# First attention of a decoder layer: each step's values product in two halves of 256 queries, one half and one unit of maxima behind each pair of scores

## The reference, cut to what is touched

```python
attn = jnp.einsum('bhqd,bhkd->bhqk', q, k) * SCALE
diff = pos[None, :] - pos[:, None]
diff = jnp.where(diff > 0, 0.0, diff)
attn = attn + diff[None, :, :] * slopes[:, None, None] * MAX_BIAS
w = jax.nn.softmax(attn, axis=-1)
out = jnp.einsum('bhqk,bhkd->bhqd', w, v)
```

## Time and profile before

| | us |
|---|---|
| median of 3 runs | 1965.26 (1962.78 to 1966.6) |
| the profiled execution | 1962.87 |
| its span, first to last instruction | 1961.1 |
| of it the 16 groups of the first attention | some 766 (160 to 926) |

### The profile page before, as it was taken

One profiled execution on the slowest core, in us unless ns is written; L12 is line 12 of the kernel. 1 busy time (PEld: TensorE's weight loads), 2 busy tenths in 40 slices (PEclk: granted clock), 3 DMA queues, 4 the chain that ended last, 5 costly groups with the idle time before them and its releaser, 6 DMA issues. The chain is left out here.

```text
span 1961.1 us, 37426 instructions
## 1 busy us (share of the span) xinstructions
PE 1681.3 (86%) x15124; PEld 1148.3 (59%) x15124; DVE 1374.4 (70%) x2318; ACT 994.8 (51%) x1602; POOL 475.1 (24%) x312
## 2 busy tenths in 40 slices
PE   8758999999999999997584898875993999999970
PEld 7734444444444444442573776764772888999970
DVE  7687888888888888880675878762332777777736
ACT  5325777777777777776252545452442433333310
POOL 6440000000000000000432633320453344444430
PEclk9957999999999999999797999987996999999995
DMA  7877444444444444400654112103212343333225
GB/s 248 222 198 183 65 65 65 68 65 65 65 65 65 65 65 64 65 9 10 209 197 137 65 55 75 54 11 135 77 52 81 96 91 92 89 90 90 36 31 173
DMA packets 128567, 178.93 MB, mean 91 GB/s; under 512 B 30144, under 2 KB 95056, under 8 KB 127380
## 3 DMA queue, kind: packets, MB, share of 16 engines
q1 hardware_dynamic: 114964, 154.57, 34.4%
q0 software_dynamic: 13440, 22.07, 5.4%
HBM read 110.49 MB, written 69.47 MB: 92 GB/s over the span
## 5 line engine op out<-in xcount | busy, mean ns | idle before, releaser
L638 DVE TENSOR_REDUCE att_row_max<-att_ring 128x2 f32<-128x1024 f32 x512 | 602.2, 1220 | 108.9 <-PE att_ring L704 57.1
L622 ACT ACTIVATE att_w_exp<-att_s_ps 128x512 f32<-128x512 f32 x1024 | 548.2, 596 | 232.3 <-PE att_s_ps L747 157.3
L774 PE MATMUL att_a_ps<-att_w_exp,att_v_group 128*32 128x512 f32 x2048 | 273.6, 606 | 0.2 <-ACT att_w_exp L622 0.2
L733 PE MATMUL att_s_ps<-att_q_stack,att_k_stack 62*128 62x512 f32 x640 | 182.0, 481 | 0.0
L560 POOL COPY att_eyes<-keep_slope_eye 128x384 bf16<-128x384 bf16 x16 | 8.1, 510 | 641.9 <-PE att_s_ps L747 632.6
L733 PEld LDWEIGHTS att_s_ps<-att_q_stack,att_k_stack 62*128 62x128 f32 x640 | 84.4, 184 | 124.0 <-ACT att_w_exp L622 113.0
L2050 POOL DMA_INDIRECT x_scr<-ex_y,ex_home x64 | 105.1, 1642 | 181.2 <-DVE ex_y L2139 166.6
L2094 ACT ACTIVATE ex_hid<-ex_h_ps,ex_b 128x512 f32<-128x512 f32 x128 | 87.3, 686 | 115.5 <-DVE ex_h_lo L2149 61.9
L704 PE MATMUL att_ring<-att_k_stack,att_q_stack 60*128 60x512 f32 x640 | 131.5, 451 | 6.2 <-DVE att_att L665 3.2
L747 PE MATMUL att_s_ps<-att_eyes,keep_past_bf 64*128 64x64 bf16 x3840 | 133.8, 193 | 0.0
L2149 DVE TENSOR_TENSOR ex_h_lo<-ex_hid,ex_h_hi 128x512 fp32r<-128x512 f32 x128 | 130.5, 1019 | 4.4
(11 more groups left out here) (270 smaller groups left out, 3810.2 us busy)
## 6 DMA issues: line engine op xcount, KB each, us to landing
first_w_raw<-ew SPq DMA_DIRECT2D x16, 1024.0 KB, 7.5
att_k_stack<-qk_scr SPq DMA_DIRECT2D x120, 128.0 KB
keep_k_stack<-qk_scr SPq DMA_DIRECT2D x72, 128.0 KB
rows_scr<-att_zeros POOLq DMA_DIRECT2D x8, 1040.0 KB, 22.9
ex_rows<-rows_scr SPq DMA_DIRECT2D x16, 520.0 KB, 4.8
cr_q<-q_scr SPq DMA_DIRECT2D x16, 512.0 KB, 5.3
att_q_stack<-qk_scr SPq DMA_DIRECT2D x60, 128.0 KB
qk_scr<-qkv_t_hi SPq DMA_DIRECT2D x7, 1024.0 KB, 4.3
```

The source lines that it names most:

```text
L622: nc.scalar.activation(w_exp[(STEPS * g.n + st) % SETS][h][:, :], s_ps[v % BANKS][:, :], ACT.Exp).then_inc(exp_done, 1)
L638: nc.vector.tensor_reduce(out, ring[place.slot][:, :, :], AX.X, ALU.max).then_inc(ring_free, 1)
L733: ins = nc.tensor.matmul(s_ps[v % BANKS][:, :], ks[g.buf][rows, c, j, kt * P:(kt + 1) * P], qs[g.buf][rows, j, c * CH:(c + 1) * CH], start ...
L774: ins = nc.tensor.matmul(a_ps[32 * h:32 * h + 32, :], vg[g.buf][:, kt, h * VW:h * VW + 32], w_exp[(STEPS * g.n + st) % SETS][h][:, :], sta ...
```

## The change

`values` gets a parameter `part`. For `kt == 0` part 0 does the whole block as before (512 columns) and part 1 does nothing; for the other seven key tiles of a chunk each part multiplies 256 of the 512 query columns, and the step is counted on `pv_done` by the last one. `old_values` chooses the group as before. In the step, part 0 follows the first pair of scores (with the transpositions behind it), then comes the first unit of maxima, then the second pair of scores, part 1, and the second unit. ScalarE's accumulator copies in steps 1 and 9 move from behind head 1's exponential to behind head 2's, because the last values now end later. Nothing else differs; the ring's order is the same.

```diff
-                        if st == 1 and h == 1 and has_last:
+                        if st == 1 and h == 2 and has_last:
                             copy_acc(g.plus(-1), 1)
-                        if st == 9 and h == 1:
+                        if st == 9 and h == 2:
                             copy_acc(g, 0)
...
-            def values(g, st):
+            def values(g, st, part):
                 c, kt = divmod(st, KT)
-                pe.wait_ge(exp_done, TILES * g.n + 4 * st + 4 + BANKS)
-                if st == 0:
-                    pe.wait_ge(v_ready, g.n + 1)
-                if kt == 0:
-
-                    pe.wait_ge(acc_done, 2 * g.n + c + 1)
+                if part == 0:
+                    pe.wait_ge(exp_done, TILES * g.n + 4 * st + 4 + BANKS)
+                    if st == 0:
+                        pe.wait_ge(v_ready, g.n + 1)
+                    if kt == 0:
+                        pe.wait_ge(acc_done, 2 * g.n + c + 1)
+                elif kt == 0:
+                    return
+                cols = slice(0, CH) if kt == 0 else slice(part * CH // 2, (part + 1) * CH // 2)
                 for h in range(HG):
-                    ins = nc.tensor.matmul(a_ps[32 * h:32 * h + 32, :], vg[g.buf][:, kt, h * VW:h * VW + 32],
-                                           w_exp[(STEPS * g.n + st) % SETS][h][:, :], start=(kt == 0), stop=(kt == KT - 1))
-                ins.then_inc(pv_done, 1)
+                    ins = nc.tensor.matmul(a_ps[32 * h:32 * h + 32, cols], vg[g.buf][:, kt, h * VW:h * VW + 32],
+                                           w_exp[(STEPS * g.n + st) % SETS][h][:, cols], start=(kt == 0), stop=(kt == KT - 1 and part == 1))
+                if kt == 0 or part == 1:
+                    ins.then_inc(pv_done, 1)
+
+            def old_values(g, st, has_last, part):
+                if st > 1:
+                    values(g, st - 2, part)
+                elif has_last:
+                    values(g.plus(-1), STEPS + st - 2, part)
...
                     score_pair(g, st, 0)
-                    if st > 1:
-                        values(g, st - 2)
-                    elif has_last:
-                        values(g.plus(-1), STEPS + st - 2)
+                    old_values(g, st, has_last, 0)
...
+                    if with_max:
+                        max_pair(n, 2 * st, PLACES[g.n, "max", 2 * st])
                     score_pair(g, st, 2)
+                    old_values(g, st, has_last, 1)
                     if with_max:
-                        for i in range(2):
-                            max_pair(n, 2 * st + i, PLACES[g.n, "max", 2 * st + i])
+                        max_pair(n, 2 * st + 1, PLACES[g.n, "max", 2 * st + 1])
...
             for st in (STEPS - 2, STEPS - 1):
-                values(last, st)
+                for part in range(2):
+                    values(last, st, part)
```

## The result

| | before | after |
|---|---|---|
| median, us | 1964.41 (4 runs, 1962.78 to 1966.6) | 1980.76 (4 runs, 1976.27 to 1982.43) |
| profiled execution, us | 1962.87 | 1982.43 |
| its span, us | 1961.1 | 1980.6 |
| ratio | | 1.0079 (95%: 1.0059 to 1.0099) |

The change costs 0.8%, some 16 us; the forecast was 13.5 us more. The forecast of 1978 lies 12.7 above its own base of 1965.26. From the first to the last instruction of the attention stage the trace has 810.1 us before and 826.6 after: +16.4. The remaining 3.1 us of the two spans lie outside it, 2.0 ahead of it and 1.1 behind it, in code that is the same; executions of one kernel differ by as much (1962.78 to 1966.6 before).

A forecast was written before the change was run, and what follows sets the result against it. TensorE's order was taken to set the time. Full groups +19.2, the last group -6.0 and its final blocks +0.3 gave +13.5 us on 1962.87, that is 1976.4, forecast as 1978 for the median; range 1958 to 1998.

The forecast's parts named there:

- The price of a half, 0.57: TensorE, half block of values to the next work: 0.57 us, two halves 1.14, plus 0.14 a step.
- The rest of the 0.27 of a halved step: TensorE's unwaited stream: beyond the halves' 0.14, plus 0.09 or 0.10 for another entry into values, plus 0.03 behind values.
- Halved steps wait for nothing: Both score pairs of a halved step find their exponentials finished, and VectorE's maxima keep up: no waiting.
- The covers of 0.15 and 0.17 us: First pair's second matmul: work ahead outlasts the exponential's release by 0.15 off the diagonal, 0.17 on it.
- The waits that go: First-pair waits regained per full group: 1.08 in steps 4 to 8, 0.97 in steps 12 to 15.
- Steps 2 and 3: Whole values in step 2, then a 0.53 wait in step 3: together 7.48 against 6.97, plus 0.5.
- Steps 9 to 11: Steps with tops, accumulator transposition and a wait behind whole values: together 9.22 against 9.03, plus 0.2.
- then the unit waits for a ring slot until 1.43: Step 9, behind the tops' transposition: the unit of maxima gets its ring slot at 1.43, the step taking 3.09.
- fourteen steps: -6.0: Last group, without maxima: half the values in the exponential loop makes it 0.43 shorter, 2.18 instead of 2.61; -6.0 us.
- halves cost nothing extra: Rival: a halved step's price is 0 instead of 0.27, giving 1922 us; chance 0.04.
- Partly hidden: Rival: second entry or tail is cheaper before a unit, 0.13 a halved step, giving 1949 us; chance 0.10.
- The wait stays: Rival: exponentials start later and the first pair waits on, giving 2017 or 1998 us; chance 0.11.

The follow-up runs named there:

- e2: kernel before with each step's values, except the first key tile's, in two halves directly behind each other: 1965.81 us (before 1963.7).
- e6: changed kernel with first-attention exponentials over 256 of 512 columns, part of the computation left out: 1978.16 us, a full group 48.73.
- e5: kernel before with first-attention exponentials over 256 of 512 columns, part of the computation left out: 1932.33 us, a full group 45.62.
- e8: changed kernel with the next group's first tops transposed in step 12 instead of step 9: 1971.74 us, ratio to before 1.0049.

## Why the prediction was right, point by point

- **The price of a half, 0.57:** measured 0.57 in the halved steps of every kernel here, whatever follows the half, where that doesn't wait. That the price belongs to halves that stand apart, and not to short matmuls, was only assumed; e2 shows it.
- **The rest of the 0.27 of a halved step:** the sum holds in the middle, its parts don't, so that this is luck in part. The prediction added 0.09 for a second entry into values and 0.03 for an exit, and put the moved units at nothing. In step 13 the two pairs take 1.12 in the changed kernel (0.60 and 0.52) where 0.62 + 0.52 = 1.14 was laid out for the order before, so the second entry adds nothing. The units take 0.75 apart where they took 0.61 together: that is the other 0.14. Step 11 of the changed kernel has its second pair at 0.33 (0.34 in the earlier trace rows) and its units at 0.34 and 0.47, 0.81 where the earlier trace rows has 0.60:

```profile
542.68 0.50 PE L704 MATMUL att_ring<-att_k_stack,att_q_stack 60*128 60x512 f32 x2
543.02 0.40 PE L733 MATMUL att_s_ps<-att_q_stack,att_k_stack 62*128 62x512 f32 x2
543.35 0.64 PE L778 MATMUL att_a_ps<-att_w_exp,att_v_group 128*32 128x256 f32 x8
543.91 0.50 PE L704 MATMUL att_ring<-att_k_stack,att_q_stack 60*128 60x512 f32 x2
544.25 0.29 PE L712 MATMUL att_ring<-att_eyes,keep_past_bf 64*128 64x64 bf16 x8
544.38 0.48 PE L733 MATMUL att_s_ps<-att_q_stack,att_k_stack 62*128 62x512 f32 x2
```

 Why units apart cost more than together, by up to 0.21, no run shows.
- **Halved steps wait for nothing:** right for exponentials, by the timeline and by e6. The covers of 0.15 and 0.17 us held.
- **The waits that go:** steps 4 to 8 came out at 13.11 against 13.35. The 1.08 of waits counted there was too little: e5's steps that wait for nothing take 2.29 and 2.39 there, not the 2.40 laid out, so some 1.4 could be won (an estimate from these two). Steps 12 to 15 came out at 12.45 against 12.49.
- **Steps 2 and 3:** 7.39 against 7.48, with the wait of 0.5 where it was forecast. **Steps 0 and 1:** 6.48 against 6.45.
- **Steps 9 to 11:** 9.67 against 9.22; this is the mis-sized term. The step that failed is "then the unit waits for a ring slot until 1.43": VectorE was laid out as free from step 8's units on, and its three operations on the tops behind step 7 were forgotten. The wait lasted until 1.85. Step 10 came out at 3.34 against 3.18, and not by inheritance from step 9, since in e8 step 9 has no such wait and step 10 takes 3.34 all the same: its last unit carries corrections (0.40 instead of 0.31), and its values start 0.47 behind the pair instead of 0.41, 0.14 behind the end of the accumulator's copy, for which the prediction had "nothing". Step 11 was 0.11 shorter than laid out.
- **A full group:** +1.43 against +1.3. That it is so near is luck in part, since steps 9 to 11 were 0.45 too short and steps 4 to 8 0.24 too long.
- **The last group:** -5.0 to the stage's end, against -5.7. The step that failed is "fourteen steps: -6.0". Off the diagonal the loop is as laid out (2.17 against 2.18). On the diagonal it is 2.72 against 2.56 (2.99 less the 0.43), because another loop was overlooked: a pair's second matmul waits for the first exponential of the pair just before, and on the diagonal no exponential of a pair starts before the corrections of both its heads. The rows show it, exponentials at 932.08 and 933.43, 1.35 apart, and so twice a step:

```profile
932.08 1.08 ACT L622 ACTIVATE att_w_exp<-att_s_ps 128x512 f32<-128x512 f32 x2 [0.27 <-PE att_s_ps L747]
932.56 0.66 PE L733 MATMUL att_s_ps<-keep_q_stack,keep_k_stack 62*128 62x512 f32 x2
...
933.43 1.09 ACT L622 ACTIVATE att_w_exp<-att_s_ps 128x512 f32<-128x512 f32 x2 [0.26 <-PE att_s_ps L747]
```

 Steps 3 and 11 there wait longer behind their whole values too (3.40 and 2.84; with the first tile halved 2.73 and 2.18).
- **The rivals:** "halves cost nothing extra" is excluded by the changed kernel's own rows, and e2 shows the only place where it holds, which is with nothing between the halves. "Partly hidden" at 0.13 a step is excluded by the 0.20 to 0.35 between e5 and e6. "The wait stays" is excluded by e6. Of the signs that the prediction named, "no step off the diagonal under 2.6" failed by a little, step 8 having 2.54, and the last group took 39.1 instead of 37.3.

In the stage the forecast was +13.5 and the traces show +16.4: a full group was 0.14 too cheap (15 of them, 2.1 us) and the last group's gain 0.7 too large.

## What to carry to other kernels

Before splitting work to fill another engine's wait, count what each piece costs when it stands apart, as the distance between starts in rows of the same kind, and count it for the work that the pieces push apart too; the split pays only where the wait at that place is longer. A rearrangement that removes waits in most steps leaves the exceptions (a whole block, a slot taken by something else) as its largest losses, so lay those out first, with every small operation of the other engine in them. Where one stretch of a loop has less work on the bound engine, like the last group here, the same edit can pay there alone.

## What the runs showed of the hardware that was not expected

Two blocks of four float32 matmuls of 256 columns (eight rows each), directly behind each other on the same four column tiles, took 1.00 us, to the hundredth what one block with 512 columns took; only with other work behind each did they take 0.57, and a transposition whose row has the same 128*32 as theirs counted as other work. Two units of maxima took 0.60 to 0.71 together and 0.75 to 0.81 with values and scores between them.
